# The order of the two passes inside each gate and up product block

## What is computed

```python
h = jax.nn.silu(jnp.einsum('ech,ehi->eci', inp, wg)) * jnp.einsum('ech,ehi->eci', inp, wu)
out = jnp.einsum('eci,eih->ech', h, wd)
```

## Time and profile before

| what | value |
|---|---|
| median of three runs | 2394.57 us |
| span of the profiled execution, first to last instruction | 2381.5 us |
| TensorE matmul busy | 2354.5 us, 99% of the span |
| VectorE, ScalarE, GpSimdE busy | 70%, 58%, 59% |
| mean granted TensorE clock | 0.996 of full speed |
| time on the last chain | 93% TensorE |

### The profile page before, as it was taken

How to read it: one execution, slowest core, us unless ns; L and a number is a source line. 1 busy time by engine, 2 the same in 40 slices (tenths; PEclk the granted TensorE clock), 3 DMA queues, 4 the chain that set the end, 5 groups by cost and what they waited for, 6 DMA issues and landing times.

```text
span 2381.5 us, 35318 instructions
## 1 busy us (share of the span) xinstructions
PE 2354.5 (99%) x12762; PEld 2074.8 (87%) x12762; DVE 1664.0 (70%) x2874; ACT 1369.5 (58%) x2256; POOL 1414.4 (59%) x1032
## 2 busy tenths in 40 slices
PE   8989999999999999999999999999999999999999
PEld 5778888888888888888888888888889999999999
DVE  6888888888888878888888788888862244444443
ACT  5767777777767767777777777777761211111110
POOL 4027888787778777777777777777710122222222
PEclk9999999999999999999999999999999999999999
DMA  9998999999998999989989989899876354444441
GB/s 343 385 328 283 285 291 272 288 282 287 278 298 279 284 282 280 281 277 287 282 274 288 284 276 282 275 290 280 274 196 132 87 140 130 130 130 130 128 121 60
DMA packets 250352, 582.33 MB, mean 245 GB/s; under 512 B 82745, under 2 KB 106682, under 8 KB 250178
## 3 DMA queue, kind: packets, MB, share of 16 engines
q1 hardware_dynamic: 183202, 401.18, 51.5%
q0 software_dynamic: 55584, 160.02, 26.0%
q10 hardware_dynamic: 11392, 18.88, 2.2%
HBM read 456.51 MB, written 123.45 MB: 244 GB/s over the span
## 4 chain that ended last, share of the span: by engine, by line
PE 93%; POOL 2%; DMA 2%; issue 1%; DVE 1%; ACT 0%; ACTq 0%; SPq 0%; DVEq 0%; POOLq 0%
PE ps L808 25%; PE ps L821 21%; PE ps L920 17%; PE ps L807 12%; PE ps L878 5%; PE ps L804 4%; PE ps L677 2%; PE ps L913 2%; PE ps L805 2%; POOL Xg L573 1%; PE ps L687 1%; PE ps L893 1%; DMA Xg<-yd,idx 1%; PE ps L700 1%; PE ps L699 0%
## 5 line engine op out<-in xcount | busy, mean ns | idle before, releaser
L808 PE MATMUL ps<-XX,HR 128*128 128x512 f32 x2688 | 961.0, 397 | 0.0
L573 POOL DMA_INDIRECT Xg<-yd,idx x504 | 663.4, 1316 | 160.5 <-issue 152.7
L807 PE MATMUL ps<-XX,LR 128*128 128x256 f32 x2688 | 751.2, 279 | 0.1
L1540 DVE TENSOR_TENSOR LR<-raw,HR 128x1536 fp32r<-128x1536 f32 x384 | 657.3, 1752 | 3.7 <-ACT HR L1075 3.6
L808 PEld LDWEIGHTS ps<-XX,HR 128*128 128x128 f32 x2688 | 505.9, 188 | 104.4
L1075 ACT ACTIVATE HR<-raw 128x1536 fp32r<-128x1536 f32 x384 | 556.5, 1478 | 11.8 <-DMA raw<-in_L_ffn_wd 8.9
L807 PEld LDWEIGHTS ps<-XX,LR 128*128 128x128 f32 x2688 | 508.3, 189 | 18.3 <-DVE LR L1540 0.7
L595 POOL DMA_INDIRECT accd<-ot,toki x128 | 253.0, 1977 | 149.9 <-ACT ot L1129 127.7
L920 PE MATMUL ps<-MH,xT 128*128 128x392 f32 x1536 | 335.8, 344 | 0.0
L821 PE MATMUL ps<-LR,hH 128*128 128x512 f32 x768 | 303.3, 395 | 0.0
L821 PE MATMUL ps<-HR,hH 128*128 128x512 f32 x768 | 299.8, 390 | 2.9 <-DVE LR L1540 2.2
(11 more groups left out here) (214 smaller groups left out, 3226.1 us busy)
## 6 DMA issues: line engine op xcount, KB each, us to landing
raw<-in_L_ffn_wd SPq DMA_DIRECT2D x128, 768.0 KB, 4.8
raw<-in_L_ffn_wg SPq DMA_DIRECT2D x126, 768.0 KB, 7.3
raw<-in_L_ffn_wu SPq DMA_DIRECT2D x126, 768.0 KB, 6.9
yd<-yrow ACTq DMA_DIRECT2D x32, 512.0 KB, 6.7
x<-accd SPq DMA_DIRECT2D x32, 512.0 KB, 5.2
out<-osb SPq DMA_DIRECT2D x31, 512.0 KB, 3.0
xt<-in_x SPq DMA_DIRECT2D x25, 512.0 KB, 8.2
accd<-xt SPq DMA_DIRECT2D x25, 512.0 KB, 6.6
```

The source lines that it names most:

```text
L573: eng.indirect_dma_start(Xg[:, c, q, :], None, yd4, bass.IndirectOffsetOnAxis(ap=idx4[:, e % 4, i:i + 1], axis=0))\
L807: eng.matmul(bank(out, 0, CAP), wl, xx[:, 0:CAP], start=False, stop=False)
L808: mm = eng.matmul(bank(out), wh, xx, start=False, stop=(k == 7))
L1540: eng.tensor_tensor(LR[:, (n + 2) % NHL, :], raw[:, n % NRAW, :], HR[:, (n + 2) % NHL, :].bitcast(F32), ALU.subtract).then_inc(s_L, 1)
```

## The change

In every block the high product now stands first at every k and the low one second. So the first and the later contraction blocks no longer need two cases. The bank is opened by the high product of k = 0, as before, and the last matmul of a block, which carries the signal, is now a low product of 256 columns in place of a high one of 512.

```diff
-                            if k == 0:
-                                eng.matmul(bank(out), wh, xx, start=True, stop=False)
-                                eng.matmul(bank(out, 0, CAP), wl, xx[:, 0:CAP], start=False, stop=False)
-                            else:
-                                eng.matmul(bank(out, 0, CAP), wl, xx[:, 0:CAP], start=False, stop=False)
-                                mm = eng.matmul(bank(out), wh, xx, start=False, stop=(k == 7))
+                            eng.matmul(bank(out), wh, xx, start=(k == 0), stop=(k == 7))
+                            mm = eng.matmul(bank(out, 0, CAP), wl, xx[:, 0:CAP], start=False, stop=(k == 7),
+                                            skip_group_check=(k == 7))
                     mm.then_inc(s_up, 1)
```

## The result

The changed kernel takes 2397.52 us against 2393.4 us for the kernel before (medians of 17 runs each): ratio 1.0019, 95% interval 1.0012 to 1.0026. It is slower by 0.19%, about 4 us, where 8 us less were forecast. In a later session the same two kernels gave 2386.62 (11 runs) and 2382.21 us (23 runs), ratio 1.0020 (1.0011 to 1.0028).

The account below looks back on a forecast made before the run. TensorE was taken to bound the kernel at 25.02 us per expert; the fast cadence throughout would save 0.14 us, 8.4 us over 60 experts, so 2394.6 − 8.4 = 2386.2 us, range 2381 to 2403.

Parts of the forecast that it names:

- TensorE sets the pace, and only the distances count: From the fourth expert on, 25.02 us per expert; a change counts only through distances between matmul starts, 60 times over.
- The waits behind a low product, and the block's end, cost nothing: Bank and LR waits costed at nothing, at most 34.5 us if cover were lost; block-end signal same within 0.01 us.
- A stretch keeps its cadence, and what changes is the cadence of 48 pairs: Gate and up blocks: each cadence holds to its block's end; without seams, 48 pairs per expert set the change's price.
- the no-change rival: Matmuls cost by size and load, or bank borders switch cadence; six blocks stay 16.78 us, time 2394.6; chance 0.27.
- a sign of being wrong: Prediction wrong if strict alternation finds a cadence that the trace of the kernel before does not have.
- the fast one that was forecast: Gate and up pairs at about 0.348 us, put at 16.64 us per expert, saving 8.4 us over 60; chance 0.5.
- After `down` the first block is the fast one too, and the slow cadence in the expert shown arises only behind a seam. So I take the fast cadence: Choice of cadence for all six gate and up blocks: 16.64 us against 16.78, saving 0.14 us per expert.
- low-low seam: Low behind low at each block's start, 0.12 then 0.11 us; removing it was said to save nothing directly.
- The fallback row: Third expert, clock just back: two pairs from 261.04 to 261.74 take 0.70 us, 0.35 each, near the fast end.
- The slow rival: Slow cadence throughout gate and up blocks: 16.99 us per expert, 0.21 more, 12.6 us in all, time 2407.2; chance 0.2.
- the two cases of a single cadence: Gate and up blocks all fast, 2386.2 us (chance 0.5), or all slow, 2403 to 2408 us (chance 0.2).
- the formula that the prediction used: Matmul distance is columns over 2.4 GHz plus 2.5 ns: 0.216 and 0.109 us, 0.325 per pair, no change from order.

Follow-up runs that it names:

- the kernel with the seam at k = 3: Changed kernel, but low first at k = 1 and 2 of each expert's first gate block; ratio 1.0018 to the kernel before, times in two groups.
- the chosen fast kernel: Experts 0-5 ordered as before, 6-7 as changed, 8-63 low first at k = 1, 2 of first gate block; 2372.53 against 2382.63 us before, ratio 0.9963.

## Why the prediction was wrong

*TensorE sets the pace, and only the distances count*: right. No wait was added, VectorE and ScalarE were as busy as before, and 60 × 0.078 = 4.7 us accounts for the whole result.

*The waits behind a low product, and the block's end, cost nothing*: right, by the timeline and the idle columns above.

*A stretch keeps its cadence, and what changes is the cadence of 48 pairs*: right, and it is what the change is about. The blocks did not go on alternating with the bank, as the no-change rival had it, nor did each matmul cost by its size alone. The 117 230 is a cadence that the steady part of the trace before does not have, which the prediction had named as a sign of being wrong; but it costs as much as the fast one that was forecast, so the failure lies elsewhere.

*"After `down` the first block is the fast one too, and the slow cadence in the expert shown arises only behind a seam. So I take the fast cadence"*: this step failed. The first block behind `down` was fast because its low-low seam made it so at that entry. Entered at H236 without that seam, the same stream goes L116 H225 and is slow from its second pair on. The seam was taken for the disturbance and was the cure, though not everywhere: entered at H226 to H229, the same low-low seam is followed by the slow cadence. The trace of before had no stretch behind `down` without a seam, so it could not decide this. The prediction also took every expert to be entered alike. In the changed kernel the entry goes round between H227, H236 and H229, by what the expert ahead left, and only H229 leads to the fast cadence. The fallback row, two pairs at 0.35 where the clock came back, reads L117 H235 L116 H230 to the nanosecond. That is how the third cadence begins, which the changed kernel's steady part has only in one expert of three.

*Sizes.* A fast expert is 24.885 us where 24.88 was forecast, 0.135 less than before and not 0.14. A slow one is 25.20, 0.185 more and not 0.21; some 0.015 of it is the longer `down`, which the prediction held at 8.24. Two slow and one fast make +0.078 on average. The slow rival had the mechanism and lacked only that every third expert escapes. The time lies inside the stated range, between the two cases of a single cadence, but on the other side of no change than forecast. That is luck: it fell into the band that was kept for no change (2390 to 2399), by a mixture that none of the cases had.

The Trainium skill (TensorE: Matmul & The Clock Gate, Back-to-back issue gap) gives the distance by the columns alone: the formula that the prediction used, which the section calls the isolated gap, and about 131 ns for 512 columns in a sustained stream of weight loads and matmuls. The runs agree with neither: 512 columns took 223 to 242 ns in the steady gate and up products of the changed kernel, and an expert's same 96 matmuls take from 16.644 to 16.953 us by what stood ahead of them.

Open: what in TensorE makes three cadences, and why a seam leads from one to another. Only their order and lengths are shown, and behind which distance a high-high seam leads to which. The four quick times of the kernel with the seam at k = 3 have no profile; that they are the pace of the chosen fast kernel is argued from their size, and from that kernel, whose last 56 experts have the same order and keep the fast pace once they are in it.

## What to carry to other kernels

Where one engine has run without a wait for hundreds of microseconds, compare blocks of equal work in the trace, to the nanosecond. If they differ, the order of instructions may be worth something by itself: here it was −0.4 to +0.5% without any added product, and the tidier order was not the faster one. Here the pace had memory: it was dealt at irregular places, by what had come before, and kept until the next. A kernel can then be quick or slow by how its start went, which may show as two groups of times, and here an order that forgets the start made the pace choosable. Compare stretches in the steady part and not spans of single profiles: the spans here differed by 12.4 us where the change was 4.

## Not expected of the hardware

- The steady part repeats within a nanosecond: 25.020 us for each expert of the kernel before from the fifth on, and 24.885, 25.206, 25.202 in two executions of the changed kernel in different sessions.
- Every repeating length in these traces is a whole multiple of 6.667 ns, which is 16 cycles of 2.4 GHz (why is open): 25.020 is 3753 of them, 24.900 is 3735, 25.140 is 3771, 25.180 is 3777, 50.120 (two experts) is 7518, and 75.293 (three) is 11294. The rounds of the cadences are too: 693.3 ns for two pairs is 104, 1060 ns for three is 159. At the half clock, in experts 0 and 3 of the kernel before, the distances were 213 and 427 ns, columns over 1.2 GHz with nothing added, and no cadence was to be seen.
- The same pair of matmuls, 256 and 512 columns, costs 0.3467 or 0.3533 us, and in these traces the difference lasts as long as nothing irregular comes.
